# A fused attention and FFN kernel: the keys of a group loaded in eight transfers instead of four

## The chip, the cores and the metric

The kernel runs on one core of one Trainium2 chip. The time is the device time of one execution in microseconds (us). The kernel before took 2485.4 us in the median of three runs (2484.12 to 2489.93).

## The reference

One post-norm layer with two halves: attention, then a feed-forward net with 4-bit weights. The change is in the attention, whose reference is, cut to what matters:

```
B, S, HIDDEN, N_HEADS, KV_HEADS, HEAD_DIM = 2, 1024, 512, 32, 8, 128     # 4 query heads share one key head
q = (x @ Wq.T).reshape(B, S, 32, 128).transpose(0, 2, 1, 3)              # then rotary embedding
k = keys of 8 heads, part of the dimensions with rotary embedding, part from c_kv @ Wupk.T
v = (c_kv @ Wupv.T).reshape(B, S, 8, 128).transpose(0, 2, 1, 3)
scores = einsum('bhqd,bhkd->bhqk', q, repeat(k, 4)) * scale              # causal mask
attn = softmax(scores, axis=-1)
out = einsum('bhqk,bhkd->bhqd', attn, repeat(v, 4))
x = layernorm(x + out.reshape(B, S, 4096) @ Wo.T)
x = layernorm(x + ffn(x))
```

Every fp32 operand of a product is split into a high and a low part, and a product is three matmuls (high by high, high by low, low by high).

## The kernel before, in words

The program has three stages. Stage A (until about 230 us) computes the keys `k_d`, the values `v_d` and the split inputs `xs_d` in DRAM. Stage B (until about 2050 us) is the attention. Stage C is the feed-forward net.

Stage B goes over 16 groups, one for each pair of batch and key head. The first is written out (`"first"`), fourteen are the turns of a loop (`"loop"`), and the last is written out again (`"last"`); a short `"end"` finishes what is left over. The keys of a group are the tile `kt` (128 partitions x 2 parts x 1024 columns, fp32, 1 MB). There is a single such tile, so the keys of a group can only be loaded when the last scores of the group before it have been read from it.

A group is 32 steps (`CELLS`), step c for query tile `i = c // 4` and head `h = c % 4`. In step c TensorE computes the scores of 128 queries against the first `128 * (i + 1)` keys, because of the causal mask: steps 0 to 15 read only the columns 0 to 511 of `kt`, and steps 16 to 31 read columns from both halves (`scores_width`). VectorE masks and takes the maximum, ScalarE does exp and the normalisation, TensorE transposes the probabilities of the cell three steps back (`LAG = 3`), and ScalarE and VectorE take these out of PSUM.

Between these TensorE works off a list of other products, `FILL`, in a fixed order and with a fixed number of matmuls a step (`ROOM`): `pv` (probabilities by values), `wo` (output projection), `q0` and `q1` (queries of the first and the second 512 rows, from the inputs `xs` and the weights `wq`). Of interest here: step 0 of a turn has the 21 matmuls of `pv` 6, and `turn_of` of the TensorE program issues them ahead of the first scores. Those of `wo` 5 follow from step 1 on. `q1` 0 may start from step 2 on.

All DMAs around the change are issued by SyncE (SP), in program order, on one queue. At step 0 of a turn its program is:

```
if step == 0 and turn in ("loop", "last"):
    sp.wait_ge(s_done, CELLS * it)      # all scores of the group before
    load_k(it)                          # kt, 1 MB
for _bk, kind, a, g in finished(step, turn, 1):
    if kind == "q0" and a == 3:
        sp.wait_ge(q_mm, 8 * (it + g) + 4)
        load_xs(it + g, 1)              # xs, 2 MB, right behind load_k; for q1 0
```

TensorE waits for `k_in` in `scores` (L1053, at c = 0) and for `xs_in` in `queries` (at its first matmul). Four of these loads of 32 partitions each make `load_k`, because the rows of `k_d` lie in four parts. The loads for group 0 are issued in stage A's last block, followed there by the loads of `vt`, of the tables, of the weights `wraw` and of `xs`.

Of the kernel before, what the change touches and what calls it, by code (L numbers as in the profile page):

```python
# [36 lines left out]
TB = 512  # L37
# [200 lines left out]
def program(nc, x, xT, wqT, wkrT, wdkT, wupkT, wupvT, woT, w13p, s13p, w2p, s2p, cosT, sinT, shifts, out):  # L238

    xs_d = nc.dram_tensor("xs_d", [NBLK, P, 2, DC, TB], F32).ap()  # L240
    k_d = nc.dram_tensor("k_d", [GROUPS // 4, 4, P, 2, S], F32).ap()
    v_d = nc.dram_tensor("v_d", [GROUPS, P, QT, 2, HD], F32).ap()
    y_d = nc.dram_tensor("y_d", [B, QT, P, D], F32).ap()
    x1_d = nc.dram_tensor("x1_d", [NBLK, 4, P, D], F32).ap()

    attention(nc, x, xT, wqT, wkrT, wdkT, wupkT, wupvT, woT, cosT, sinT, xs_d, k_d, v_d, y_d)
    stage_c(nc, w13p, s13p, w2p, s2p, shifts, y_d, x1_d, out)


def words(ap):  # L250

    return ap.bitcast(F32)


def three_pass(nc, out, pairs, first=0, end=None):


    every = [(lhsT(a), rhs(b)) for lhsT, rhs in pairs for a, b in PASSES]
    for n in range(first, len(every) if end is None else end):
        ins = nc.tensor.matmul(out, *every[n], start=(n == 0), stop=(n == len(every) - 1))  # L260
    return ins
# [3 lines left out]
def attention(nc, x, xT, wqT, wkrT, wdkT, wupkT, wupvT, woT, cosT, sinT, xs_d, k_d, v_d, y_d):  # L265


    with ExitStack() as ctx:
# [3 lines left out]
        def at(offset, name, shape, dt):  # L272
            return nc.alloc_sbuf_tensor_at(name, shape, dt, offset=base + offset)

        def sem(name):
            return ctx.enter_context(nc.semaphore(name))
# [19 lines left out]
        kt = at(0, "b_kt", [P, 2, S], F32R)  # L296
# [45 lines left out]
        a_k_out, a_xs_out, a_y_out = sem("a_k_out"), sem("a_xs_out"), sem("a_y_out")  # L342
        a_v_out = [sem("a_v_out0"), sem("a_v_out1")]
        tab_in, masked = sem("b_tab_in"), sem("b_masked")
        k_in, v_in, xs_in = sem("b_k_in"), sem("b_v_in"), sem("b_xs_in")
        w_in = [sem("b_w_in0"), sem("b_w_in1")]
        w_hi, w_lo = sem("b_w_hi"), sem("b_w_lo")
        y_in, y_out = [sem("b_y_in0"), sem("b_y_in1")], [sem("b_y_out0"), sem("b_y_out1")]
# [21 lines left out]
        def a_count(t, g):  # L370

            return GROUPS_A * t + g + 1
# [14 lines left out]
        def scores_width(i):  # L387


            w = P * (i + 1)  # L390
            return [(0, max(w, 256))] if w <= 512 else [(0, w // 2), (w // 2, w)]
# [32 lines left out]
        def _(sp):  # L424
# [49 lines left out]
                sp.dma_start(wraw[:, h % 2], woT[(it % KV) * GQ + h]).then_inc(w_in[h % 2], 16)  # L474

            def load_k(it):
                for part in range(4):
                    sp.dma_start(words(kt[32 * part:32 * part + 32]), k_d[it // 4, part, bass.ds((it % 4) * 32, 32)])\
                        .then_inc(k_in, 16)

            def load_v(it):
                sp.dma_start(words(vt[:]), v_d[it]).then_inc(v_in, 16)
# [12 lines left out]
            def turn_of(it, turn):  # L495
                for step in steps_of(turn):
                    if step == 0 and turn in ("loop", "last"):
                        sp.wait_ge(s_done, CELLS * it)
                        load_k(it)
# [3 lines that stand above are left out]
                            load_xs(it + g, 1)  # L503
                        if kind == "q1" and a == 3 and turn != "last":
                            sp.wait_ge(q_mm, 8 * (it + g) + 8)
                            load_xs(it + g + 1, 0)
                        if kind == "pv" and a == 7 and turn != "end":
                            sp.wait_ge(pv_done, QT * (it + g + 1) + PV0)
                            load_v(it + g + 1)
                    for _bk, kind, a, g in finished(step, turn, 2):  # L510
                        if kind == "va":
                            a_store_v(END, a)
                        if kind == "wo":
                            store_y(it + g, a)
                            if a + 2 < QT:
                                load_y(it + g, a + 2)
                            elif turn != "end":
                                load_y(it + g + 1, a + 2 - QT)
                    if turn != "end" and step in WO_LOADS:
                        load_wo(it, WO_LOADS.index(step))  # L520
                    if turn in ("first", "loop") and step in WQ_LOADS:
                        load_wq(it + 1, WQ_LOADS.index(step))
# [8 lines left out]
            sp.wait_ge(a_w_lo, len(LATE))  # L531
            sp.wait_ge(a_k_out, 16 * 8 * 2 + a_OUT0)
            load_k(0)
            for p in range(2):
                sp.wait_ge(a_v_out[p], 16 * 4 * 2 + a_OUT0)
# [463 lines left out]
        def _(pe):  # L999
# [47 lines left out]
            def scores(it, c):  # L1047
                i, h = c // GQ, c % GQ
                if c == 0 and type(it) is int and it == 0:
                    pe.wait_ge(a_bank_free, a_count(END, VG + V_LATE - 1) + a_FREE0)  # L1050
                if c == 0:
                    pe.wait_ge(k_in, 64 * (it + 1))
                pe.wait_ge(q_lo, 8 * it + 4 * (i // 4) + h + 1 + QLO0)  # L1053
                pe.wait_ge(sc_done, CELLS * it + c + 1)
                if c in (16, 17):
                    pe.wait_ge(ot_lo, QT * it + c - 16 + 1)
                q = (i % 4) * P
                for k, (a, b) in enumerate(scores_width(i)):
                    last = three_pass(nc, sps[c % 2][:, 512 * k:512 * k + b - a],
                                      [(lambda p: qs[:, i // 4, h, p, q:q + P], lambda p: kt[:, p, a:b])])  # L1060
                last.then_inc(s_done, 1)
# [82 lines left out]
            def turn_of(it, turn):  # L1144
                for step in range(CELLS):
                    parts = plan_of(turn).spread[step]
                    here, cell = cell_at(step, it, turn), cell_at(step - LAG, it, turn)
                    if step == 0:
                        fill(it, turn, parts)
                        parts = []  # L1150
                    ts = pieces(cell[1]) if cell else []
                    shares = cut(parts, SHARES[len(ts)])
                    for job in PE_ORDER[part_of(step)]:
                        if job == "scores":
                            if here:
                                scores(*here)
                        elif job == "fill":
                            if shares:
                                fill(it, turn, shares.pop(0))
                        elif job < len(ts):  # L1160
                            transposes(*cell, ts[job])
# [560 lines left out]
```

## Time and profile before

| | |
|---|---|
| median of three runs | 2485.4 us |
| the profiled execution | 2487.67 us |
| its span in the trace | 2485.9 us |
| TensorE busy | 2408.9 us, 97% of the span |
| ScalarE, VectorE, GpSimd busy | 64%, 57%, 23% |
| granted TensorE clock, mean | 0.991 of full speed |
| one turn of the loop | about 113.7 us |

The span runs from the first to the last instruction; the execution's own time is 1.8 us longer. Busy shares are those of the whole span. In the rows, PE is TensorE's matmuls and PEld its weight loads, DVE is VectorE, ACT is ScalarE, POOL is GpSimd, SPq is the queue of SyncE. In square brackets stands how long the engine was idle ahead of the row and what ended it. Matmuls overlap: each begins before the one ahead has left the array, so that the stated start of a row can lie before the end of the row ahead of it.

### The profile page before, as it was taken

What the parts mean: (1) busy time and instruction counts of PE and PEld (TensorE: products, weight loads), DVE (VectorE), ACT (ScalarE), POOL (GpSimd) and SP (SyncE); (2) the same over time, 40 slices, a digit from 0 to 9 for tenths busy, and PEclk for the clock granted to TensorE, in tenths of its full rate; (3) what the DMA queues carried; (4) which work ended last, traced back from release to release, by engine and by line L of the source; (5) the groups of instructions that cost most, each with busy time, mean ns of one, the idle gap of its engine ahead of it and who ended that gap; (6) DMA issues with size and microseconds to landing.
All of it is one profiled execution on the core that took longest, in us unless ns stands there. A gap on an engine that the chain in (4) does not pass through costs nothing. (4 is left out here: it accounts for less than half of the span.)

```text
span 2485.9 us, 40420 instructions
## 1 busy us (share of the span) xinstructions
PE 2408.9 (97%) x12028; PEld 1997.4 (80%) x12028; DVE 1425.2 (57%) x3333; ACT 1597.1 (64%) x3213; POOL 571.6 (23%) x445
## 2 busy tenths in 40 slices
PE   8999999999999999999999999999999996899998
PEld 7887888888888888888888888888888875678886
DVE  4334656566666666566666666666666666842332
ACT  4223878787777878787777878787877762332211
POOL 3002313223231323132222313231322202300000
PEclk9999999999999999999999999999999998999999
DMA  7767333324242323233242424232332316520100
GB/s 266 276 217 272 124 98 111 114 93 155 67 155 82 131 82 133 93 110 115 96 156 72 148 80 132 90 124 93 110 122 89 116 42 190 153 78 34 51 34 17
DMA packets 110979, 293.38 MB, mean 118 GB/s; under 512 B 10832, under 2 KB 27728, under 8 KB 101648
## 3 DMA queue, kind: packets, MB, share of 16 engines
q1 hardware_dynamic: 110928, 292.73, 35.4%
q8 instruction: 28, 0.46, 0.1%
q14 instruction: 23, 0.19, 0.0%
HBM read 208.80 MB, written 88.08 MB: 119 GB/s over the span
## 5 line engine op out<-in xcount | busy, mean ns | idle before, releaser
L924 DVE TENSOR_TENSOR b_pt<-b_tps,b_pt 128x512 fp32r<-128x512 f32 (+3 forms) x768 | 427.1, 556 | 370.7 <-ACT b_pt L767 369.6
L752 ACT ACTIVATE b_sc<-b_sc,b_rinv 128x896 f32<-128x896 f32 (+7 forms) x512 | 397.0, 775 | 294.4 <-DVE b_rinv L914 290.9
L260 PE MATMUL b_sps<-b_kt,b_qs 128*128 128x512 f32 (+4 forms) x2304 | 501.8, 344 | 10.2 <-DMA b_kt<-k_d 10.1
L260 PEld LDWEIGHTS b_sps<-b_kt,b_qs 128*128 128x128 f32 x2304 | 403.0, 188 | 72.4 <-issue 18.9
L260 PE MATMUL b_ps<-b_xs,b_wq 128*128 128x512 f32 x1536 | 442.3, 407 | 2.6 <-issue 2.6
L260 PE MATMUL b_ps<-b_pt,b_vt 128*128 128x512 f32 x1584 | 436.4, 402 | 2.5 <-DVE b_ys L935 2.5
L260 PE MATMUL b_ps<-b_wo,b_ot 128*128 128x512 f32 x1536 | 423.7, 406 | 1.8 <-DVE b_ys L935 0.6
L767 ACT ACTIVATE b_pt<-b_tps 128x512 fp32r<-128x512 f32 (+3 forms) x768 | 364.5, 475 | 63.7 <-PE b_tps L1068 63.0
L746 ACT ACTIVATE b_sc<-b_sc,b_nmax 128x896 f32<-128x896 f32 (+7 forms) x512 | 392.7, 767 | 1.0 <-DVE b_nmax L906 1.0
L1068 PE MATMUL b_tps<-b_ident,b_sc 128*128 128x128 f32 x2304 | 377.4, 274 | 8.9 <-DVE b_pt L924 5.7
L906 DVE CUSTOM_DVE_ANT_0 b_sc<-b_sps,b_mask 128x896 f32<-128x896 f32 (+7 forms) x512 | 380.2, 743 | 0.0
L1068 PEld LDWEIGHTS b_tps<-b_ident,b_sc 128*128 128x128 f32 x2304 | 287.7, 140 | 97.3 <-DVE b_pt L924 15.8
L260 PEld LDWEIGHTS b_ps<-b_pt,b_vt 128*128 128x128 f32 x1584 | 285.8, 189 | 50.8 <-DVE b_ys L935 2.9
L260 PEld LDWEIGHTS b_ps<-b_xs,b_wq 128*128 128x128 f32 x1536 | 275.1, 190 | 47.7 <-issue 3.0
L260 PEld LDWEIGHTS b_ps<-b_wo,b_ot 128*128 128x128 f32 x1536 | 270.7, 189 | 48.4 <-DVE b_qf L888 4.1
L598 POOL TENSOR_TENSOR b_sw<-b_sw,b_sin 128x512 f32<-128x512 f32 x128 | 165.5, 1293 | 498.5 <-ACT b_sw L720 498.5
L602 POOL TENSOR_TENSOR b_qs<-b_qf,b_qs 128x512 fp32r<-128x512 f32 x124 | 160.3, 1293 | 482.3 <-ACT b_qs L726 482.3
L914 DVE RECIPROCAL b_rinv<-b_rsum 128x1 f32<-128x1 f32 x512 | 81.1, 158 | 194.5 <-PE b_sps L260 182.9
L888 DVE TENSOR_TENSOR b_qf<-b_ps,b_cos 128x512 f32<-128x512 f32 x128 | 88.5, 691 | 98.2 <-ACT b_sw L720 54.2
L260 PE MATMUL c_a<-c_xs,c_w 128*128 (+3 forms) x528 | 135.3, 407 | 8.4 <-DVE c_hb L1508 4.2
L611 POOL TENSOR_TENSOR b_wo<-b_wraw,b_wo 128x512 fp32r<-128x512 f32 x64 | 83.0, 1297 | 239.7 <-ACT b_wo L740 239.7
L1616 PE MATMUL c_y<-c_w,c_hs 128*128 128x512 f32 (+1 forms) x528 | 129.6, 395 | 7.1 <-DVE c_hs L1514 7.1
(137 smaller groups left out, 2386.9 us busy)
## 6 DMA issues: line engine op xcount, KB each, us to landing
b_xs<-xs_d SPq DMA_DIRECT2D x32, 2048.0 KB, 9.1
b_ys<-y_d SPq DMA_DIRECT2D x128, 256.0 KB, 2.7
y_d<-b_ys SPq DMA_DIRECT2D x128, 256.0 KB, 2.5
k_d<-a_ks SPq DMA_DIRECT2D x32, 512.0 KB, 4.2
v_d<-a_vs SPq DMA_DIRECT2D x32, 512.0 KB, 3.0
b_kt<-k_d SPq DMA_DIRECT2D x64, 256.0 KB, 4.5
b_vt<-v_d SPq DMA_DIRECT2D x16, 1024.0 KB, 4.8
b_wraw<-in_wqT SPq DMA_DIRECT2D x64, 256.0 KB, 2.7
```

What stands on the lines that cost most here:

```text
L260: ins = nc.tensor.matmul(out, *every[n], start=(n == 0), stop=(n == len(every) - 1))
L598: nc.gpsimd.tensor_tensor(sw[:], sw[:], sinq[:, blk * TB:blk * TB + TB], ALU.mult).then_inc(sin_done, 1)
L602: nc.gpsimd.tensor_tensor(qs[:, blk, h, LO], qf[:], qs[:, blk, h, HI], ALU.subtract).then_inc(q_lo, 1)
L611: nc.gpsimd.tensor_tensor(wo[:, h, LO], wraw[:, h % 2], wo[:, h, HI], ALU.subtract).then_inc(w_lo, 1)
L746: nc.scalar.activation(sc[:, slot, 0:w], sc[:, slot, 0:w], ACT.Exp, bias=nmax[:, slot:slot + 1], scale=-1.0, accum_out=rsum[:, slot:slot + ...
L752: nc.scalar.activation(sc[:, slot, 0:w], sc[:, slot, 0:w], ACT.Copy, scale=rinv[:, slot:slot + 1])\
L767: nc.scalar.activation(pt[:, u % PT_UNITS, HI, 0:nj, h * P:(h + 1) * P], tps[n % 2][:, 0:nj], ACT.Copy)\
L888: nc.vector.tensor_tensor(qf[:], banks[bk], cosq[:, blk * TB:blk * TB + TB], ALU.mult)\
L906: nc.vector.tensor_tensor_reduce(out=like_banks(sc[:, slot, 0:w], i), in0=both_banks(sps[c % 2], i), in1=like_banks(mask[:, S - w:S], i), ...
L924: nc.vector.tensor_tensor(pt[:, u, LO, 0:nj, h * P:(h + 1) * P], tps[n % 2][:, 0:nj], pt[:, u, HI, 0:nj, h * P:(h + 1) * P], ALU.subtract) ...
L1068: last = nc.tensor.transpose(tps[n % 2][:, j], sc[:, c % S_RING, (j0 + j) * P:(j0 + j + 1) * P], ident[:])
L1616: last = nc.tensor.matmul(yps[t][:], hs[0:w, f % 2, a, t * P:(t + 1) * P], w2[0:w, b, f], start=(f == 0 and k == 0), stop=(f == FT - 1 and ...
```

## The change

`load_k` issues eight transfers instead of four: first the columns 0 to 511 of the four 32-partition parts (each 32 x 2 x 512 elements, 128 KB, in runs of 2 KB), then the columns 512 to 1023. Each half counts on a semaphore of its own. `scores` waits for the first half at step 0 and for the second at step 16.

```
-        k_in, v_in, xs_in = sem("b_k_in"), sem("b_v_in"), sem("b_xs_in")
+        k_in, v_in, xs_in = [sem("b_k_in0"), sem("b_k_in1")], sem("b_v_in"), sem("b_xs_in")
...
             def load_k(it):
-                for part in range(4):
-                    sp.dma_start(words(kt[32 * part:32 * part + 32]), k_d[it // 4, part, bass.ds((it % 4) * 32, 32)])\
-                        .then_inc(k_in, 16)
+
+                for half in range(2):
+                    cols = slice(TB * half, TB * half + TB)
+                    for part in range(4):
+                        sp.dma_start(words(kt[32 * part:32 * part + 32, :, cols]),
+                                     k_d[it // 4, part, bass.ds((it % 4) * 32, 32), :, cols]).then_inc(k_in[half], 16)
...
             def scores(it, c):
-                if c == 0:
-                    pe.wait_ge(k_in, 64 * (it + 1))
+                if c in (0, 16):
+                    pe.wait_ge(k_in[c // 16], 64 * (it + 1))
```

What SyncE issues at the start of a loop turn, before. L478 is `load_k`, L485 is `load_xs`; an `ISA` or `REGISTER_ALU` row computes an address or holds a wait:

```order
L478 ISA [waits b_s_done]
L478 REGISTER_ALU
L478 DMA b_kt<-k_d 32x2048
L478 ISA
L478 DMA b_kt<-k_d 32x2048
L478 ISA
L478 DMA b_kt<-k_d 32x2048
L478 ISA
L478 DMA b_kt<-k_d 32x2048
L502 ISA
L485 ISA [waits b_q_mm]
L485 DMA b_xs<-xs_d 128x4096
```

And of the changed kernel the last twelve rows of the same place, from the fourth transfer of the keys on (L481 is `load_k`, L488 is `load_xs`); ahead of them stand the wait for `b_s_done` and three transfers of the same form:

```order
L481 DMA b_kt<-k_d 32x2x512
L481 ISA
L481 DMA b_kt<-k_d 32x2x512
L481 ISA
L481 DMA b_kt<-k_d 32x2x512
L481 ISA
L481 DMA b_kt<-k_d 32x2x512
L481 ISA
L481 DMA b_kt<-k_d 32x2x512
L505 ISA
L488 ISA [waits b_q_mm]
L488 DMA b_xs<-xs_d 128x4096
```

The load of `xs` has moved behind four more transfers; nothing else on SyncE changes its place.

On TensorE no matmul moves. Around the scores of step 16 (b_sps is their PSUM tile) its rows in a loop turn were:

```order
L260 MATMUL b_ps<-b_xs,b_wq 128x512 x8
L1054 REGISTER_ALU [waits b_q_lo]
L1056 REGISTER_ALU [waits b_sc_done]
L260 MATMUL b_sps<-b_kt,b_qs 128x320 [waits b_ot_lo]
L260 MATMUL b_sps<-b_kt,b_qs 128x320 x5
```

and are now:

```order
L260 MATMUL b_ps<-b_xs,b_wq 128x512 x8
L1057 REGISTER_ALU [waits b_q_lo,b_k_in1]
L1059 REGISTER_ALU [waits b_sc_done]
L260 MATMUL b_sps<-b_kt,b_qs 128x320 [waits b_ot_lo]
L260 MATMUL b_sps<-b_kt,b_qs 128x320 x5
```

One wait, for the second half of the keys, has come to three others.

## Rows read from the trace of the kernel before

**Rows 1.** The page, busy time and share of the span by engine.

```profile
PE 2408.9 (97%) x12028; PEld 1997.4 (80%) x12028; DVE 1425.2 (57%) x3333; ACT 1597.1 (64%) x3213; POOL 571.6 (23%) x445
```

**Rows 2.** Waits of TensorE, whole span: total us, times, longest us.

```profile
PE b_sps L260 <- DMA b_kt<-k_d: 10.1, 14, 1.0
...
PE b_tps L1068 <- DVE b_pt L924: 5.7, 20, 0.6
```

**Rows 3.** Timeline, loop turn 1: start us, us, engine, line, operation, count.

```profile
337.44 1.91 SPq L478 DMA_DIRECT2D b_kt<-k_d  x4
...
339.70 0.35 SPq L485 DMA_DIRECT2D b_xs<-xs_d  x1
...
343.42 0.39 PE L260 MATMUL b_ps<-b_pt,b_vt 128*128 128x512 f32 x1
344.80 0.62 PE L260 MATMUL b_sps<-b_kt,b_qs 128*128 128x256 f32 x3 [0.98 <-DMA b_kt<-k_d]
...
345.89 0.60 ACT L767 ACTIVATE b_pt<-b_tps 128x512 fp32r<-128x512 f32 x1 [4.17 <-PE b_tps L1068]
...
350.87 0.63 PE L260 MATMUL b_ps<-b_xs,b_wq 128*128 128x512 f32 x2
```

**Rows 4.** Timeline, step 16 of loop turn 1: a boundary without a wait.

```profile
384.15 2.10 PE L260 MATMUL b_ps<-b_xs,b_wq 128*128 128x512 f32 x8
386.09 1.04 PE L260 MATMUL b_sps<-b_kt,b_qs 128*128 128x320 f32 x6
```

**Rows 5.** Timeline, the last group's start.

```profile
1933.34 1.98 PE L260 MATMUL b_ps<-b_pt,b_vt 128*128 128x512 f32 x8
...
1935.38 0.41 PEld L260 LDWEIGHTS b_sps<-b_kt,b_qs 128*128 128x128 f32 x3 [0.50 <-DMA b_kt<-k_d]
1935.39 0.62 PE L260 MATMUL b_sps<-b_kt,b_qs 128*128 128x256 f32 x3
```

**Rows 6.** From issue to landing, first and fourth key transfer, turn 1.

```profile
DMA to landing us min/median/max: 3.4/3.4/3.4
...
DMA to landing us min/median/max: 5.5/5.5/5.5
```

**Rows 7.** From issue to landing: xs of turn 1, then of turn 2.

```profile
DMA to landing us min/median/max: 9.8/9.8/9.8
...
DMA to landing us min/median/max: 9.4/9.4/9.4
```

**Rows 8.** Stretches of turn 1; the last two columns are DMA share and GB/s.

```profile
342.00:343.00 1.00, 1.00 (x6) 0.81 (x6) 0.00 (x0) 0.00 (x0) 1.00 (x1) 1.00 1.09 238
...
347.00:348.00 1.00, 1.00 (x5) 0.79 (x5) 0.29 (x1) 1.00 (x3) 0.00 (x0) 1.00 1.15 492
```

**Rows 9.** DMA issues of whole tiles: count, KB each, median us to landing.

```profile
b_ys<-y_d SPq DMA_DIRECT2D x128, 256.0 KB, 2.7
...
k_d<-a_ks SPq DMA_DIRECT2D x32, 512.0 KB, 4.2
...
b_kt<-k_d SPq DMA_DIRECT2D x64, 256.0 KB, 4.5
```

**Rows 10.** Timeline, loop turn 2.

```profile
451.31 1.89 SPq L478 DMA_DIRECT2D b_kt<-k_d  x4
453.55 0.35 SPq L485 DMA_DIRECT2D b_xs<-xs_d  x1
...
458.27 0.61 PE L260 MATMUL b_sps<-b_kt,b_qs 128*128 128x256 f32 x3 [0.59 <-DMA b_kt<-k_d]
...
464.33 0.62 PE L260 MATMUL b_ps<-b_xs,b_wq 128*128 128x512 f32 x2
```

**Rows 11.** From issue to landing, the 29 loads of xs from 330 us on.

```profile
DMA to landing us min/median/max: 7.6/9.2/9.8
```

**Rows 12.** Timeline, end of stage A, ScalarE.

```profile
194.06 1.30 ACT L732 ACTIVATE b_wq<-b_wraw 128x512 fp32r<-128x512 f32 x2 [3.96 <-DMA b_wraw<-in_wqT]
197.96 1.17 ACT L690 ACTIVATE a_ks<-a_kf 128x512 fp32r<-128x512 f32 x2 [2.61 <-DVE a_kf L863]
```

## The prediction

> **What bounds the kernel now.** I read the busy times first: TensorE is busy 2408.9 us of 2485.9, 97%, and the next engine, ScalarE, 64% [rows 1]. So time is saved where TensorE works less or waits less, and this change removes no work. Next the waits of TensorE [rows 2]: in the attention the largest is the one for the keys, 10.1 us in 14 waits, the longest 1.0. The second, for VectorE's `b_pt`, is 5.7 us in 20 and has nothing to do with loads. Then the timeline of a turn's start, where that wait is made. In turn 1 the four key transfers are issued from 337.44, TensorE starts the last matmul of its filling work at 343.42 and the first scores at 344.80, after 0.98 us idle for the keys [rows 3]. In turn 2 it is 0.59 [rows 10]; the fourteen lie between 0.48 and 0.98. The last group starts almost without idle time, but its weight load waits 0.50 for the keys too [rows 5].
>
> **What the change removes.** The idle time is not the whole price of a wait. Where TensorE doesn't wait, a row starts before the one ahead has ended: at step 16 of turn 1 the row from 384.15 ends at 386.25 and the next starts at 386.09, 0.16 earlier [rows 4]. After a wait this overlap is lost as well. So turn 1 pays 0.98 + 0.16 = 1.14, turn 2 0.59 + 0.16 = 0.75, the fourteen together 10.1 + 14 x 0.16 = 12.3, and the last group (1935.39 less the end of the row ahead, 1933.34 + 1.98 = 1935.32) 0.07 + 0.16 = 0.2. Sum at stake: 12.5 us. Without the wait turn 1 wants its keys at 344.80 - 1.14 = 343.66, which is 6.2 us after the first issue; in turn 2 it is 458.27 - 0.75 - 451.31 = 6.2 too.
>
> When will the first half be there? Before, the first 256 KB landed 3.4 us after their issue and the fourth, issued about 1.6 later, after 5.5, that is 7.1 after the first issue [rows 6]. The three later transfers took 7.1 - 3.4 = 3.7 us, 1.2 each. The first half is as many bytes as two of these transfers, so by bytes it lands at 3.4 + 1.2 = 4.6. It can also be bound by the issues: four take 1.91 us [rows 3], the last begins 1.5 after the first, and with 3.4 to landing it is there at 4.9. Both are at least 1.3 us before 6.2. The rows of the transfers are now 2 KB long instead of 8 KB, and the trace has no load of 2 KB rows into 32 partitions. From below: nothing, since `b_ys`, 256 KB in rows of 2 KB, lands in 2.7 us, and `k_d`, written in 2 KB rows, moves 512 KB in 4.2, both faster per byte than the keys' 4.5 for 256 KB [rows 9]. From above: a transfer of half the bytes takes as long as a whole one, 1.2 us, and the half lands where the whole did, at 7.1 (a rival below). I take the bytes, since these rows are of the same length. So the wait at step 0 goes: -12.5 us.
>
> The Trainium skill, in "SBUF — State Buffer", section "Door 1: The DMA port swizzle", says that a transfer's bandwidth goes by the number of the 16 ports that its partitions reach, and 32 neighbouring partitions reach 8, half of 435 GB/s. The trace agrees: while keys are moved the DMA engines are fully busy at 238 GB/s, and while `xs` goes to 128 partitions at 492 [rows 8]. By that rule cutting the columns leaves the rate alone, as I assumed from the landings.
>
> **What it adds.** First, the second half: it is wanted at step 16, at 386.09 in turn 1 [rows 4], 48.7 us after the first issue, and lands within 10. Its wait joins three others on TensorE that are passed at that place without any idle time [rows 4]; 0, at most a few hundredths of a us a turn, 0.5 in all.
>
> Second, four more issues on SyncE, 1.91 us or, with the address work between, about 2.1. Behind them stands the load of `xs`: issued 453.55 - 451.31 = 2.24 after the first key issue [rows 10], now about 4.3. It has a reader: the first `q1` matmul at 350.87 and 464.33 [rows 3, 10]. Before, `xs` landed at 339.70 + 9.8 = 349.5 and 453.55 + 9.4 = 462.95 [rows 7], 1.4 us early in both. Now TensorE comes 1.14 and 0.75 earlier, which leaves 0.2 and 0.6; over the fifteen groups the smallest is turn 1's 0.2, the next 0.3, the largest 0.8. Does `xs` land later? The DMA engines are busy without a gap from the keys into `xs` [rows 8]; I read it that `xs` queues behind the keys, and a transfer that queues doesn't care that it is issued 2 us later. The bytes ahead of it are the same. The limit is its time without a queue: the shortest of 29 is 7.6 [rows 11], which puts the landing at 4.3 + 7.6 = 11.9 after the first key issue; before it was 11.6 to 12.1, and TensorE now wants it at 12.3 (464.33 - 0.75 - 451.31; turn 1: 350.87 - 1.14 - 337.44 = 12.3). So it is just hidden in most turns and may cost 0.1 to 0.2 in a few. I take +0.3 us for all. The transfers behind `xs` on SyncE begin with a store of `b_ys`, which waits for a sum that VectorE makes some steps later, and aren't late.
>
> Third, group 0's keys are issued in stage A's last block, with loads behind them. The first of them that an engine is waiting for are the weights `wraw`, at 194.06, and ScalarE then splits them for 1.30 us. If they came 2.1 us later, that would end at 197.5, still before ScalarE's next job at 197.96 [rows 12]. 0.
>
> **Sum.** -12.5 + 0.3 = -12.2 us, in a profiled execution of 2487.67: 2475.5. The median of the runs is 2485.4, 2.3 below that execution, so I forecast 2485.4 - 12.2 = 2473.2 us, 0.49% faster. About 0.3%, 7.5 us, is what a measurement of this kernel can tell from no change.
>
> **Rivals.** (a) `xs` becomes the wait, and the kernel is slower. If `xs` keeps its 9.5 us from issue to landing, as if it didn't queue, it lands at 4.3 + 9.5 = 13.8 after the first key issue, and `q1` 0 wants it at 12.3: a wait of 1.5 plus the lost overlap of 0.16, 15 times, 25 us, against 12.5 gained. The time is 2485.4 + 12.5 = 2497.9. It decides from a landing at 13.0 on, where the new wait is as large as the old. For it: the loads of `xs` that don't follow keys are not much faster, 7.6 at least. Against it: the busy DMA engines between [rows 8].
> (b) Transfers cost by the piece. Then the first half lands at 7.1 like the whole before, the wait stays, and the four others delay `xs` too. The time is 2485.4, no change, or that of (a) if `xs` slips too. Against it: rows 9. The Trainium skill speaks for it: "DMA: Bandwidth & Descriptors", section "Anatomy of one DMA — SWDGE (gpsimd) path", fits 2.0 us and the bytes at 436 GB/s to one transfer, and "Rules for kernel authors" there asks to coalesce small ones. Paid one after another that would be, as an estimate by the page, 4 x 2.3 = 9.2 us for the first half alone. The trace disagrees for these loads: their fixed parts overlap, four land 1.2 us apart [rows 6].
> (c) Part of it is given back. The stall lets VectorE and ScalarE catch up once a turn, and without it the waits for `b_pt` [rows 2] grow. If half comes back, the time is 2485.4 - 6 = 2479.4. Against it: ScalarE, the busiest after TensorE, has stood idle 4.17 us when the stall is over [rows 3], so the stall gives it nothing that it lacks, and it waits for TensorE there, so that it moves along.
>
> **Chances.** The forecast (10 to 13.5 us gained) 0.72, (c) 0.13, (b) without change 0.05, (a) or (b) with slower 0.07, more than 13.5 gained 0.03. Faster by over 0.3%: 0.72 + 0.03 and most of (c), 0.10, is 0.85. Within 0.3%: the rest of (c), (b), and `xs` half late, 0.09. Slower by over 0.3%: 0.06. The range goes from 2470.5 (14 us from the lost overlaps and 1 of scatter) to 2480 (into (c), with `xs` late by 0.3 a turn); the forecast's own is 2471.9 to 2475.4.
>
> **What the profile after would show.** The row of waits of TensorE for `b_kt` gone, and the first scores of a turn starting 6.2 us after the first key issue with no idle time. Eight key issues in about 4.0 us, `xs` issued 4.3 after the first, with 7.6 to 7.9 to landing instead of 9.4. No row of TensorE waiting for `b_xs`, or one under 1 us in all. A turn of 112.9 us instead of 113.7. Waits for `b_pt` near 5.7. I am wrong if a wait for `b_xs` of over 0.5 a turn appears, if the key wait keeps more than a fifth, or if the waits for `b_pt` and `b_sc` grow by several us.

## The result and the profile after

The changed kernel takes 2524.8 us in the median of four runs (2521.95 to 2528.02), the kernel before 2486.93 in four runs beside it: a ratio of 1.0152, with a 95% interval of 1.014 to 1.0164. It is 38 us slower, where 12 us less were forecast.

The profiled execution is 2524.87 us, its span 2522.8, 36.9 above the span before. The page's line of busy times (answers to [rows 1]):

```profile
PE 2428.6 (96%) x12028; PEld 2014.3 (80%) x12028; DVE 1425.4 (57%) x3333; ACT 1597.0 (63%) x3213; POOL 572.6 (23%) x445
```

TensorE has the same 12028 matmuls and is busy 19.7 us longer with them. The other engines do what they did. Its waits (total us, times, longest us; answer to [rows 2]):

```profile
PE b_ps L260 <- DMA b_xs<-xs_d: 30.1, 14, 3.3
...
PE b_tps L1071 <- DVE b_pt L927: 5.7, 20, 0.6
```

The wait for the keys is gone altogether, that for `b_pt` is what it was, and a wait of 30.1 us for `xs` has come. Turn 1 shows how (first SyncE's queue, then TensorE; answers to [rows 3]):

```profile
335.46 6.40 SPq L481 DMA_DIRECT2D b_kt<-k_d  x8
342.22 0.35 SPq L488 DMA_DIRECT2D b_xs<-xs_d  x1
```

```profile
341.66 0.52 PE L260 MATMUL b_sps<-b_kt,b_qs 128*128 128x256 f32 x3
...
346.72 1.09 PE L260 MATMUL b_ps<-b_wo,b_ot 128*128 128x512 f32 x4
351.15 1.22 PE L260 MATMUL b_ps<-b_xs,b_wq 128*128 128x512 f32 x2 [3.33 <-DMA b_xs<-xs_d]
352.17 1.05 PE L1071 MATMUL b_tps<-b_ident,b_sc 128*128 128x128 f32 x4
```

The first scores start 6.20 us after the first key issue, without idle time. But the eight issues took 6.40 us instead of the 4 that I had reckoned with, and `xs` went out at 6.76 instead of 4.3. The rows of SyncE for the keys tell why (duration of one in ns, minimum, median, maximum; before, then after):

```profile
L478 SPq DMA_DIRECT2D b_kt<-k_d x64: 315/332/811, 180.8 to 1929.8; - x64
```

```profile
L481 SPq DMA_DIRECT2D b_kt<-k_d x128: 563/564/707, 178.4 to 1968.0; - x128
```

One issue holds SyncE for 0.564 us instead of 0.332. With the address work between, the spacing is 0.78 instead of 0.52.

The last line of the first TensorE fence shows something else: two matmuls that took 0.63 in [rows 3] took 1.22. The stretches of turn 1 (the third column from the end is the granted clock):

```profile
349.00:350.00 1.00, 0.00 (x0) 0.00 (x0) 0.29 (x4) 0.00 (x0) 0.00 (x0) 0.97 0.08 33
350.00:351.00 1.00, 0.00 (x0) 0.00 (x0) 0.00 (x0) 0.00 (x0) 0.00 (x0) 0.50 0.04 16
...
356.00:357.00 1.00, 1.00 (x4) 0.84 (x4) 0.98 (x5) 0.55 (x3) 0.00 (x0) 0.62 0.00 0
357.00:358.00 1.00, 1.00 (x7) 0.83 (x6) 0.78 (x2) 0.77 (x4) 0.00 (x0) 1.00 0.00 0
```

Here the granted clock falls from 2.4 to 1.2 GHz (0.50) while TensorE stands idle, stays there while it works again, and is back at 2.4 GHz in the stretch from 357. Turn 1 is the only one of this trace in which it falls during the wait. In the ten other turns with a fall it comes 0.1 to 0.9 us after TensorE has started to work again. In turn 2 `q1` starts at 468.47 behind a wait of 1.83, and the clock falls at 469.4:

```profile
468.00:470.00 2.00, 1.53 (x8) 1.30 (x9) 0.13 (x2) 0.23 (x1) 0.00 (x0) 0.85 0.00 0
470.00:472.00 2.00, 2.00 (x9) 1.70 (x8) 0.69 (x1) 0.75 (x3) 0.00 (x0) 0.50 0.00 0
472.00:474.00 2.00, 2.00 (x10) 1.79 (x9) 1.47 (x5) 1.55 (x6) 0.00 (x0) 0.80 0.00 0
```

It fell in 11 of the 14 loop turns, behind waits of 1.79 to 3.33 us; in the three others the waits were 1.80, 1.88 and 2.15 and it didn't.

**Where the 36.9 us are.** Gained: 12.5, as forecast. Counted from the first key issue, the first scores start 12.4 us earlier in sum over the fourteen loop turns, of which 10.1 had been idle time. Lost at `xs`: 30.1 idle, 14 overlaps of 0.16, and 1.59 + 0.16 in the last group, 34.1. (For the last wait the profile names no releaser; `xs` landed 0.1 us before its end.) Lost to the clock: two loop turns with equal waits tell its price. The one from 570.63 to 686.75 waited 1.79 and the clock fell: 116.12 us. The one from 803.59 to 918.24 waited 1.80 and it did not: 114.65. So a fall costs 1.5 us, ten of them 14.7 (an estimate from this one pair), and turn 1, with the longer one, 2.7 (118.85 - 114.65 - 1.53 of longer wait). Sum: -12.5 + 34.1 + 17.4 = 39.0; the first loop turn also began 2.0 us earlier than before (335.46 for 337.44), for a reason that isn't shown, which leaves 37.0.

### The profile page after: what moved, and what is told of

Read it like the earlier page. It is cut to its first block and busy times, and to the rows that moved or that the text cites. A ratio compares the mean times of both kernels' runs of the same rounds, so it can differ in the third digit from the quotient of the medians.

```text
span 2522.8 us, 40612 instructions
## 1 busy us (share of the span) xinstructions
PE 2428.6 (96%) x12028; PEld 2014.3 (80%) x12028; DVE 1425.4 (57%) x3333; ACT 1597.0 (63%) x3213; POOL 572.6 (23%) x445
## 5 line engine op out<-in xcount | busy, mean ns | idle before, releaser
L260 PE MATMUL b_ps<-b_xs,b_wq 128*128 128x512 f32 x1536 | 453.8, 416 | 34.7 <-DMA b_xs<-xs_d 30.1
L1071 PE MATMUL b_tps<-b_ident,b_sc 128*128 128x128 f32 x2304 | 385.6, 278 | 8.9 <-DVE b_pt L927 5.7
L1071 PEld LDWEIGHTS b_tps<-b_ident,b_sc 128*128 128x128 f32 x2304 | 295.1, 143 | 98.2 <-issue 18.5
```

The costliest lines, as they stand in the source:

```text
L1071: last = nc.tensor.transpose(tps[n % 2][:, j], sc[:, c % S_RING, (j0 + j) * P:(j0 + j + 1) * P], ident[:])
```

## The experiments

Two theories at the start. *Issue*: a half transfer of the keys is dearer to issue than a whole one, which makes `xs` late; all else follows. *Data*: 2 KB runs or eight pieces keep the DMA engines busy longer. All times are medians, with the ratio to the kernel before on the same chip and its 95% interval.

**xs between the halves.** From the changed kernel:

```
 load_k(it, (0,))          # at step 0, was load_k(it)
 ...
 load_xs(it + g, 1)
+load_k(it, (1,))
```

> The changed kernel, with the load of xs issued between the two halves of the keys instead of behind both. Issue theory: a key transfer of the form 32x2x512 holds SyncE for 0.56 us (0.78 with the address work), so xs goes out 4 x 0.78 + 0.3 = 3.4 us after the first key issue instead of 6.4, lands some 8 later at 11.4, before TensorE wants it at 12.3; the wait for b_xs and the slow-clock stretch behind it go, and the 12.5 us of the key wait are gained: 2474 us, with TensorE's clock at 1.00 throughout the attention. Data theory (transfers in 2 KB runs keep the DMA engines busy longer): xs still comes late by some of it, and the time stays above that of the kernel before.

Measured: 2474.05 us, ratio 0.9954 (0.994 to 0.9967). The waits of TensorE for loads:

```profile
PE b_ps L260 <- DMA b_xs<-xs_d: 0.7, 2, 0.5
```

The same eight transfers of the same form, four of them moved behind `xs`, and the loss of 38 us is a gain of 12. The clock stays at 1.00 in every turn. The gain that I forecast was there; the change gave it away behind it. The data theory falls for the first half; the second half's data was simply no longer ahead of `xs`, so the next run was needed.

**Eight transfers by level.** From the kernel before, which waits for all at step 0:

```
-for part in range(4): ... kt[32 * part:32 * part + 32], k_d[..., ds(...)]
+for level in range(2):
+    for part in range(4): ... kt[32 * part:32 * part + 32, level], k_d[..., ds(...), level]
```

> The kernel before, with the keys loaded in eight transfers cut by level (high, low) instead of by columns: each 32x1024, 128 KB, one run of 4 KB a partition; TensorE waits for all eight at step 0. Issue-by-form theory: a transfer with one run a partition costs SyncE 0.33 us as before (0.52 with the address work), so eight take 4.1 us and xs goes out at 4.3; keys land about as before, 7 us after the first issue, xs at about 12.2, TensorE wants it at 13.0: 2485 to 2490 us, no slow clock. Issue-by-count theory (the pieces cost 0.78 each, whatever their form): keys land at 5.5 + 2.8 = 8.3, xs goes out at 6.4 and lands at 14.2, so 1.3 us more in the key wait and 0.2 in that for xs: about 2508 us or more.

Measured: 2482.88 us, 0.999 (0.998 to 0.9999). An issue took 0.316 us and `xs` went out 4.36 after the first. So it isn't the number of transfers, nor their 128 KB. It came out a little better than I expected: the keys were there earlier, and the key wait went from 10.1 us to this:

```profile
PE b_sps L260 <- DMA b_kt<-k_d: 2.2, 8, 0.5
```

**A late xs by itself.** From the kernel before:

```
 load_k(it)
+sp.wait_ge(small, 16 * 9 * (it - 1) + 1)
+for n in range(9):
+    sp.dma_start(tiny[0:32, n], sinT[0:32, 4 * n:4 * n + 2]).then_inc(small, 16)
```

> The kernel before (four key transfers, one semaphore), with nine transfers of 256 bytes put between the keys and xs on SyncE, which delay the issue of xs by about 4.2 us, to 6.4 after the first key issue, as in the changed kernel. Late-xs theory: xs lands at 6.4 + 7.8 = 14.2, TensorE wants it at 13.0; a wait of 1.2 us a turn, 15 x (1.2 + 0.16) = 20 us, and if the clock falls after such a wait, 15 x 1.3 = 20 more: 2507 to 2527. If the changed kernel's loss came from its key transfers' data and not from the issue of xs, this stays at 2487.

Measured: 2507.82 us, 1.0082 (1.0067 to 1.0097). In turn 2:

```profile
452.18 1.90 SPq L480 DMA_DIRECT2D b_kt<-k_d  x4
454.21 4.03 SPq L504 DMA_DIRECT2D b_tiny<-in_sinT  x9
458.71 0.36 SPq L487 DMA_DIRECT2D b_xs<-xs_d  x1
...
466.47 0.73 PE L260 MATMUL b_ps<-b_xs,b_wq 128*128 128x512 f32 x2 [1.15 <-DMA b_xs<-xs_d]
```

The keys' data is that of the kernel before, and the wait is there: a late issue of `xs` is enough for it. The waits were 0.88 to 1.56 us in the fourteen loop turns, and the clock stayed at 1.00 in all of them (in the last group, behind 2.45, it fell), which is why the time lies at the lower end of what was expected.

**Six instead of nine.** The run above with `range(6)`, and 6 for 9 in its wait.

> As the run with nine small transfers of 256 bytes, but with six: xs is issued at 2.2 + 6 x 0.48 = 5.1 us after the first key issue, lands 7.7 later at 12.8, and TensorE wants it at 13.0 (key wait as before). Slack theory: the first 2.9 us of delay are free, within 2 us of the kernel before: 2487. If each us of delay had its price, 2500.

Measured: 2486.38 us, 0.9997 (0.9988 to 1.0006). `xs` went out at 5.06 and landed at 12.7 to 13.3 in the loop. So the first 2.8 us of delay are free, as the slack of 1.4 us and the queue behind the keys say; this part of the prediction's working was right.

**The split of the wait undone.** From the changed kernel:

```
-if c in (0, 16):
-    pe.wait_ge(k_in[c // 16], 64 * (it + 1))
+if c == 0:
+    pe.wait_ge(k_in[0], 64 * (it + 1))
+    pe.wait_ge(k_in[1], 64 * (it + 1))
```

> The changed kernel with its eight transfers, but TensorE waits for both halves at step 0: only the split of the wait is undone. Issue theory: the last half lands 5.5 + 2.8 = 8.3 us after the first issue, so the scores start at 8.4 after a wait of 2.0; xs is issued at 6.4 and lands at 14.2, TensorE now wants it at 12.3 + 2.2 = 14.5, so no wait there. In sum 2.2 a turn instead of 0.84 before: 15 x 1.3 = 20 us more, 2506 us; if the clock falls after such a wait as after the one for xs, up to 20 more. If the loss of the changed kernel came from the place of its waits and not from its issues, undoing the split would bring it back to 2486.

Measured: 2523.68 us, 1.0138 (1.0122 to 1.0153), the same as the changed kernel within the scatter:

```profile
PE b_sps L260 <- DMA b_kt<-k_d: 31.4, 14, 2.9
```

Where TensorE waits makes no difference; it waits 30.1 us at `q1` or 31.4 at the scores. The clock fell in 12 of the 14 loop turns here, so it was the upper end of what I gave. The loss is in the loads.

**Which property of the form?** The first guess was the two runs a partition. Nine small transfers of that form:

```
-sp.dma_start(tiny[0:32, n], sinT[0:32, 4 * n:4 * n + 2])
+sp.dma_start(tiny[0:32, n, :, 0:2], sinT[0:32, 8 * n:8 * n + 8] as 32 x 2 x 4, [:, :, 0:2])
```

> As the run with nine small transfers between keys and xs, but each of the nine is of the form 32x2x2 (two runs a partition that can't be merged) instead of 32x2: same number, 512 instead of 256 bytes. Form theory: each holds SyncE for about 0.56 us instead of 0.33, so xs goes out 9 x 0.23 = 2.1 us later, at 8.6, lands at 16.3, and TensorE, which wants it at 13.0, waits 3.3 us a turn, and the clock falls in each: 2486 + 15 x (3.3 + 0.16 + 1.5) = 2560. If the price belongs to the size of a transfer or to the keys, xs goes out at 6.5 as with the other form, and the time is 2507.

Measured: 2508.11 us, 1.0086 (1.0071 to 1.0102). This guess fell. The rows of the issues, with one run a partition and with two:

```profile
L504 SPq DMA_DIRECT2D b_tiny<-in_sinT x135: 324/421/429, 339.1 to 1950.2; - x135
```

```profile
L504 SPq DMA_DIRECT2D b_tiny<-in_sinT x135: 335/427/434, 339.0 to 1951.6; - x135
```

Two runs a partition cost 6 ns. Then I looked for the price in the trace of before, and it is there, in stage A's stores:

```profile
L448 SPq DMA_DIRECT2D k_d<-a_ks x32: 533/552/1356, 38.8 to 216.4; - x32
...
L453 SPq DMA_DIRECT2D v_d<-a_vs x32: 372/376/1358, 51.9 to 266.2; - x32
```

`v_d` is written in four runs a partition and costs 0.376; `k_d` in two, and costs 0.552. In the order of instructions the first is `128x4x256`, the second `256x1x512`: the rows of `k_d` have a pitch of 1024 elements between the runs of a partition and between partitions alike, so its side is walked as 256 rows, while the other side has 128 partitions. The half loads stand to `k_d` in the same way, 64 rows to 32 partitions; that their source too is walked so is argued from the pitch, since the order of instructions shows the destination's form alone. This *shape* theory was tried in two ways.

**Small transfers with that mismatch.**

```
-sinT[0:32, 8 * n:8 * n + 8] as 32 x 2 x 4, [:, :, 0:2]
+sinT[0:64, 4 * n:4 * n + 2].rearrange("(p a) b -> p a b", a=2)
```

> As the run with nine small transfers of two runs a partition (32x2x2), but read from 64 rows of equal pitch in DRAM, so that the DRAM side can be walked as 64 rows while the other side has 32 partitions with two runs each; this is how the half key transfers stand to k_d, whose partition pitch is twice its run pitch. Shape theory: that mismatch costs SyncE 0.56 us an issue instead of 0.42, so the nine take 1.3 us longer, xs goes out at 7.9, lands at 15.6, and TensorE waits about 2.5 us a turn, with the clock falling behind most waits: 2487 + 15 x 2.66 + 15 x 1.3 = 2546. If the half key transfers are dear for their 2 KB runs or for their size, the issues stay at 0.42 and the time at 2508.

Measured: 2558.62 us, 1.0295 (1.0277 to 1.0313).

```profile
L504 SPq DMA_DIRECT2D b_tiny<-in_sinT x135: 578/594/719, 338.8 to 2000.0; - x135
```

512 bytes cost as much to issue as 128 KB. `xs` went out at 8.2, TensorE waited 41.6 us in the loop, 2.7 to 3.35 a turn, and the clock fell in 13 of the 14 turns. That is 12.6 us above my number, since the waits were up to 0.8 longer than reckoned and the clock stayed low twice as long in five turns. The turn in which it didn't fall is turn 1, with the longest wait of all, 3.35 us, up to 353.45 (the third figure from the end is the granted clock):

```profile
346.00:366.00 20.00, 16.65 (x91) 13.87 (x92) 10.71 (x37) 13.76 (x37) 3.88 (x3) 1.00 0.36 132
```

**The changed kernel without the mismatch.** 64 unused elements behind each row of `k_d` in DRAM:

```
-k_d = dram_tensor("k_d", [GROUPS // 4, 4, P, 2, S], F32)
+k_d = dram_tensor("k_d", [GROUPS // 4, 4, P, 2 * S + 64], F32)[:, :, :, 0:2 * S] as (2, S)
```

> The changed kernel with 64 unused elements added behind each partition's row of k_d in DRAM, so that the two runs of a partition and the next partition's no longer have one pitch; the transfers stay 32x2x512 in the same eight issues and the same order. Shape theory: the issues cost 0.33 to 0.42 us instead of 0.56, eight take 4.2 to 4.9 us, xs goes out at 4.5 to 5.2, lands at 12.2 to 12.9, TensorE wants it at 12.3: 2475 to 2484 us, no slow clock. If 0.56 us belongs to 2 KB runs or to three dimensions as such, nothing changes: 2525 us.

Measured: 2479.49 us, 0.9967 (0.9955 to 0.9979).

```profile
L482 SPq DMA_DIRECT2D b_kt<-k_d x128: 316/317/829, 181.6 to 1922.9; - x128
```

```profile
452.17 4.05 SPq L482 DMA_DIRECT2D b_kt<-k_d  x8
456.58 0.35 SPq L489 DMA_DIRECT2D b_xs<-xs_d  x1
...
464.66 0.73 PE L261 MATMUL b_ps<-b_xs,b_wq 128*128 128x512 f32 x2 [0.16 <-DMA b_xs<-xs_d]
```

The transfers, their order and their waits are those of the changed kernel; only the pitch in DRAM differs. It is 45 us faster. The stores to `k_d` fell from 0.552 to 0.376 too, and the order of instructions shows them as `128x2x512` now. The runs of 2 KB are the same, and in the loop the last of the keys land 6.3 to 7.3 us after the first issue instead of 8.1 to 8.6, so that the data theory falls for the second half as well.

In its issues this is the execution that the prediction described, but it gains 8.7 us and not 12.2. `xs` goes out at 4.4 and lands at 12.1 to 12.7 in the loop, 13.7 in the last group. `q1` starts 12.17 us after the first key issue where nothing holds it up (measured in the version with the second half at step 6, below) and 12.2 to 12.7 here: 3.6 us later in sum over the loop, and 1.4 in the last group. That makes 5.0 us where the forecast had 0.3, and -12.5 + 5.0 = -7.5.

**The order of the parts.** From the kernel before: `for part in (0, 2, 1, 3)`.

> The kernel before with its four key transfers in the order of parts 0, 2, 1, 3 instead of 0, 1, 2, 3. Port theory: neighbouring transfers then go to different halves of the partitions (below and above 64), the keys move faster than 238 GB/s and land up to 1 us earlier than 7.0 after the first issue; the key wait of 0.5 to 1.0 us a turn shrinks or goes: 2474 to 2482. If the rate has nothing to do with the order, 2487.

Measured: 2482.22 us, 0.9982 (0.9973 to 0.9991). The key wait went from 10.1 to 6.9 us, 1.81 of it in a single turn, and in most of the others to 0.2 to 0.5. Behind the wait of 1.81 the clock fell, here in front of the scores. The keys do land some 0.4 us earlier, so the order has a part in their rate; it isn't the 1 us that I hoped for. It doesn't bear on the loss.

**The second half at step 6.** From the version with `xs` between:

```
-load_k(it, (1,))                                   # behind load_xs at step 0
+if step == 6 and turn in ("loop", "last"):
+    load_k(it, (1,))
```

> The version with xs right behind the first half of the keys, and the second half issued only at step 6 (wanted at step 16), so that nothing follows xs. If packets of the second half slow xs down, it lands at 3.3 + 7.7 = 11.0 instead of 11.4 to 12.8, the wait of 0.48 and 0.24 us in two turns goes and 1 us is gained: 2473. If the first half, ahead of it, slows xs, it stays at 2474.

Measured: 2472.12 us, 0.994 (0.9927 to 0.9954). The last waits for loads in the loop are gone, and `xs` lands 10.9 to 11.6 after the first key issue instead of 11.5 to 12.8: it was the second half that slowed it. Its median is the lowest of all. It beats both kernels; from the one with `xs` between it can't be told apart.

## Why the prediction was wrong

**What bounds the kernel, and what the wait cost.** Right. The wait for keys was worth 12.5 us. The scores start 6.20 to 6.22 us after the first key issue in every loop turn of the changed kernel, against 6.2 forecast, and the versions in which `xs` is in time give 11.7 us (`xs` between; the interval is 8 to 15) and 14.5 us (second half at step 6; 11 to 18) against the runs beside them. The lost overlap of 0.16 a wait was real too: the scores start 12.4 us earlier in sum, and idle time accounts for 10.1 of it.

**When the first half lands.** Right in effect: there was no key wait left. Even with dearer issues, the fourth goes out at 2.3 and lands 4.9 to 5.4 after the first issue, 0.8 to 1.3 before it is wanted. Of the rates in [rows 8] the trace bears out the ratio alone: the 492 GB/s into 128 partitions, 467 in the stretch from 344 to 346, lie above the 435 that the prediction took for all ports, and 238 is about half of what was measured there.

**The second half's own wait.** Right: no row of TensorE waits for it.

**Four more issues on SyncE.** This is the step that failed. I put them at "1.91 us or, with the address work between, about 2.1", that is, at the duration of the old transfers, 0.52 apart. The new ones are 0.78 apart and the first four slow down as well: eight take 6.0 instead of 4.1, and `xs` goes out at 6.4 instead of 4.3. So `xs` goes out 4.1 us later than before and not 2.1, and the term "+0.3 us for all" became 34.1 of waits and 17.4 of slow clock. The error was to carry the price of an instruction over to one of another shape. I had asked of the shape whether its data moves as fast and looked at landings for that; I didn't ask what it costs to issue. The trace had the row, `k_d<-a_ks` at 0.552, for a transfer that I cited myself, but for its landing [rows 9].

**The margin.** It was seen, and it was thinner than I had it. I had 0.2 to 0.8 us between the landing of `xs` and its use, and put 7% on the case that it is exceeded. Three readings made it too wide: `q1` wants `xs` at 12.17 and not at 12.3; the landing was reckoned with the shortest of 29 times, 7.6, where it took 7.7 to 8.2 in the loop of the padded version; and `xs` had landed at 11.4 to 12.0 before, not 11.6 to 12.1. So even with issues as cheap as forecast, the "+0.3 us" comes to 5.0.

With so little in hand the spacing of an issue was the number on which the sign hung. Its bound from above should have been worked out as those of the landing were. The trace of before gives it: 0.55 for `k_d<-a_ks` and 0.19 of address work (0.52 less 0.33) make 0.74 apart; eight of them and the 0.16 ahead of `xs` put its issue at 6.1, and with 7.6 it lands at 13.7, 1.4 us too late. The runs gave 6.4 and 14.1 to 14.6.

**The rivals.** (a) named the right effect, `xs` as the new wait, at the right place, but for a reason that did not hold: that `xs` keeps its 9.5 us from issue to landing. It took 7.7 to 8.2 in the loop after turn 1, close to the time without a queue that the forecast had used; what made it late was its issue, at 6.4, which (a) left at 4.3. The price was put at 25 us, from a landing at 13.8; it was 14.1 to 14.6 in the turns after the first, and the clock was left out of it. Right in the effect, (a) was not right in the cause. (b), transfers by the piece, did not hold: eight of 128 KB in the by-level version delay nothing. The fixed 2.0 us a transfer that the Trainium skill fits for transfers issued by GpSimd ("DMA: Bandwidth & Descriptors", section "Anatomy of one DMA — SWDGE (gpsimd) path") do not add up for these, issued by SyncE: in the by-level version eight transfers issued within 4.1 us each land 2.2 to 4.0 us after their own issue, beside each other. (c), gains given back to VectorE or ScalarE, did not come: the waits for `b_pt` stayed at 4.2 to 5.7 us in all runs.

**The clock.** It wasn't in the prediction. In the trace of before the key waits of up to 0.98 us left it at 1.00 [rows 3, 8], and I took that for granted. A wait twice as long can be more than twice as dear: behind 1.8 to 2.3 us most turns paid another 1.5.

## What to carry to other kernels

Count the issue time of a transfer by its own shape, from a row of the trace with the same shape on both sides. A transfer cut out of a tile can be dearer to issue than the whole tile, and a pitch in DRAM that lets rows merge on one side only nearly doubled it here; some padding undid it.

When a load is split, ask what stands behind it in the same queue and how much time that has in hand; here the remedy was an order: what is wanted first is issued first, and the second half, wanted 48 us later, last.

## What the runs showed of the hardware

The issue of a DMA on SyncE took 0.316 to 0.335 us for loads of 128 or 256 KB with like shapes on both sides, 0.37 to 0.38 for stores with two or four runs a partition and like shapes, 0.42 to 0.43 for transfers of 256 or 512 bytes, and 0.55 to 0.59 where the pitch in DRAM lets that side be walked as twice as many rows as the other has partitions, whatever the bytes. Why the mismatch costs 0.17 to 0.25 us isn't shown; that it does, two runs show from both sides.

TensorE's clock stayed at 2.4 GHz in every loop turn with waits of up to 1.56 us. In the changed kernel it fell to 1.2 GHz in 11 of 14, behind waits of 1.79 to 3.33 us, and stayed there for several us of full work; in ten of these turns it fell only after TensorE had started again. The length of the wait alone doesn't settle whether it falls: 1.79 did it, 2.15 did not, and in the run with the mismatched small transfers 3.35 did not either, while 2.66 to 3.29 in the 13 other turns did. What settles it isn't shown.
